# Summing 128 estimates on TensorE and turning a ternary weight once, from DRAM: a change to the last stages of a four-block transformer kernel

## The chip, the cores and the metric

The kernel runs on one core of one Trainium2 chip. The metric is the device time of the whole launch in microseconds; the median of 3 runs of the kernel before is 1473.65 us (1471.71 to 1474.03).

## The reference

Sixteen sequences of 256 tokens of width 512 pass four residual blocks: a strided cross attention, a sparse expert layer, a plain cross attention and a quantised feed-forward layer. Only the last block is touched by the change:

```python
def _quant_act_int8(x):
    amax = jnp.maximum(jnp.quantile(jnp.abs(x), 1.0 - 0.005), 1e-5)
    s = 127 / amax
    return jnp.clip(jnp.round(x * s), -128, 127) / s

def _quant_w_ternary(w):
    gamma = jnp.mean(jnp.abs(w)) + 1e-5
    return jnp.clip(jnp.round(w / gamma), -1.0, 1.0) * gamma

def _qlinear(x, w):
    return jnp.einsum('btd,hd->bth', _quant_act_int8(x), _quant_w_ternary(w))

h = _layernorm(x, ln_g, ln_b)          # 4096 tokens x 512
h = _qlinear(h, w1)                    # 4096 x 2048
h = jax.nn.gelu(h, approximate=False)
out = x + tanh(g_ffn[1]) * _qlinear(h, w2)   # 4096 x 512
```

The second product needs the 0.995 quantile of the magnitudes of all 8.4 million values of `h` before its input can be rounded. So the kernel first writes all of `h` to DRAM, finds the quantile, and reads `h` again.

## The kernel before

The program is a row of blocks. Each block gives every engine its own list of instructions, ordered among themselves by semaphores; between two blocks all engines meet, the semaphores are cleared, and all engines meet again (L111 to L113).

`product_tops` is the first product. 4096 tokens are 32 tiles of 128. PE (TensorE) works through 32 groups: 28 wide ones (two tiles by half of the 2048 columns, 32 matmuls of 256 columns) and 4 narrow ones (one tile by all columns). Group i writes bank i mod 2 of PSUM, and PE starts group i when ACT (ScalarE) has emptied group i-2 with its Gelu (L2025, L2027). The Gelu's output lands in one of three buffers of four tiles (`third` and two thirds of `hid`). From there SP's queue writes each tile to the DRAM tensor `activations` (1 MB, L1915), and DVE (VectorE) takes the largest 8 of every 1024 values of a partition into `cand` (16 MAX8 for each tile, L2067).

Three other things run inside this stage:

- SP first issues the transposing DMAs that give `qT`, the left operand (L1899).
- POOL (GpSimd) turns the second weight w2 (512 x 2048) into -1, 0, +1 in 8 half rows of 128 x 1024: two comparisons and a subtraction (L1957 to L1960), into `signs`, which is the space of `perm`. After each second half SP issues a transposing DMA of 128 x 2048 elements into `w2T` (`turn_w2`, L1906). It stands in SP's list behind the writing of tiles 13, 17, 21 and 25 (`W2_AFTER`) and waits there for POOL; POOL waits for the transfer to land before it fills `signs` again.
- ACT estimates the quantile while the product runs. After groups 9 to 19 (`EST_GROUPS`) it does one step of a binary search in each partition (L1977 to L1982). The 128 results, one for each partition in `minus_t`, are written by SP to the DRAM tensor `estimates` (L1920), and read back, all 128 into each partition, into `allest` (L1922). Both stand in SP's list behind the writing of tile 20. After group 23 (`MEAN_GROUP`) ACT waits for them, sums them (L1992) and works out a base point in six small instructions (`average`). DVE makes a grid of 256 thresholds out of it after tile 26 (`BASE_TILE`, L2072 to L2076), ACT takes their Gelu after group 28 (`GRID_GROUP`, L2004).

`quantile2` is the second search: eight rounds of counting `cand` against a threshold, by ACT (L2109) and DVE (L2122) at once; PE sums the counts. It uses no DMA. It gives `amax2` and a count that is checked later.

`ffn` with the prefix `p8_` is the second product: read a tile of `activations`, round it, multiply it by `w2T` (16 matmuls of 512 columns for each of 32 tiles, L2324), add the residual and write the output. It ends with a check of the quantile (L2329 to L2411) that leaves `flag`.

Behind it stand two blocks that do their work only if `flag` is set, which these inputs don't: `quantile2_of_all` (a search over all values) and `ffn` with the prefix `p9_`, unrolled in full. In each of them every engine loads the flag and branches over its list (`when`, L2227).

Of the kernel before, what the change touches and what calls it, by code (L numbers as in the profile page):

```python
# [1559 lines left out]
class Search:  # L1560
# [5 lines left out]
    def __init__(self, nc, es, name, K, integers=False, sems=None):  # L1566
# [8 lines left out]
        self.tot = es.enter_context(nc.psum_tensor(f"{name}_tot", [P, 512], F32))  # L1575
# [284 lines left out]
MEAN_GROUP = EST_GROUPS[-1] + 4  # L1860
# [3 lines left out]
W2_AFTER = (13, 17, 21, 25)  # L1864


def product_tops(nc, hid, qT, w1T, gam, amax, zs, Gs, g_d, cand, K, est_d, w2, th, nth, signs, room4, w2T, base, grid):
# [9 lines left out]
    with ExitStack() as es:  # L1877
# [4 lines left out]
        bits, steps, allest = sbt("bits", [P, IBITS]), sbt("steps", [P, IBITS]), sbt("allest", [P, P])  # L1882
# [6 lines left out]
                                        + "bits_in grid_in steps_done est_own est_done est_out est_in mean_done base_own base_done grid_done w_taken w_minus w_signed w_turned w_in0 w_in1".split()))  # L1889
# [5 lines left out]
        def _(sp):  # L1895
# [8 lines left out]
            def turn_w2(k):  # L1904
                sp.wait_ge(s["w_signed"], 2 * k + 2)
                sp.dma_start_transpose(w2T[:, :, k * P:(k + 1) * P], signs[:, :]).then_inc(s["w_turned"], 16)  # L1906

            turns = 0
            for n in range(NB * WB):
                while turns < min(NPAIR, 9 + 3 * (n // 2)):  # L1910
                    turn(turns)
                    turns += 1
                j, t = divmod(n, WB)
                sp.wait_ge(s["gelu_done"], ready[n])
                sp.dma_start(g_d[:, j, t], Gs[j % R][:, t]).then_inc(s[f"spilled{j % R}"], 16)  # L1915
                if n in W2_AFTER:
                    turn_w2(W2_AFTER.index(n))
                if n == EST_GROUPS[-1] + 1:
# [3 lines left out]
                    sp.dma_start(allest[:, :], est_d.rearrange("(a p) -> a p", a=1).broadcast_to([P, P])).then_inc(s["est_in"], 16)  # L1922
            sp.wait_ge(s["w_turned"], 16 * C)
# [4 lines left out]
        def _(pe):  # L1928
            for i, (n, tiles, f0, nf) in enumerate(groups):
# [5 lines left out]
                for f in range(nf):  # L1935
                    mm = z_product(pe, bank[:, f, :], w1T, qT, f0 + f, n, tiles)
# [3 lines left out]
        def _(pool):  # L1940
# [8 lines left out]
            for i in range(2 * C):  # L1949
# [3 lines left out]
                if k and h == 0:  # L1953
                    pool.wait_ge(s["w_turned"], 16 * k)
                if i:
                    pool.wait_ge(s["w_signed"], i)
# [3 lines left out]
                pool.tensor_tensor(half, half, below[:, :], ALU.subtract).then_inc(s["w_signed"], 1)  # L1960
                if i + 2 < 2 * C:
                    load(i + 2)

        @block.scalar
        def _(act):
# [49 lines left out]
            for i, (n, tiles, f0, nf) in enumerate(groups):  # L2015
# [17 lines left out]
                if i == MEAN_GROUP:  # L2033
                    average()
# [5 lines left out]
        def _(dve):  # L2040
# [9 lines left out]
            for k in range(NPAIR):  # L2050
# [3 lines left out]
                if k == 1:  # L2054
                    dve.tensor_scalar(zs[:, 0:1], amax[:, 0:1], 1.0 / QMAX, None, ALU.mult).then_inc(s["own"], 1)
                    own()
                    dve.tensor_tensor(zs[:, 0:1], zs[:, 0:1], gam[:, 0:1], ALU.mult).then_inc(s["scale_done"], 1)
            dve.memset(level[:, :], float(NT2 - 2 * int(rank_here) + 1))
# [20 lines left out]
def quantile2(nc, cand, K, zs, cut, small, amax, base, grid):  # L2079
# [5 lines left out]
    with ExitStack() as es:  # L2085
        sbt = lambda n, sh, d=F32: es.enter_context(nc.sbuf_tensor("q2_" + n, sh, d))
        s = es.enter_context(semaphores(nc, "qb_", "consts at_ready signed counted told own found gelu_done".split()))
# [6 lines left out]
        threshold = lambda i: grid[:, widths[i]:widths[i] + 1]  # L2094

# [46 lines left out]
def quantile2_of_all(nc, flag, rows, qT, w1T, K, zs, amax):  # L2142

    rank, _, low, high = quantile_ranks(N2)
    with ExitStack() as es:
        step_names = ("z_full", "gelu_done", "counted", "step_own")
        sems = es.enter_context(semaphores(nc, "qc_", [f"q2s_{n}" for n in Search.NAMES] + list(step_names)))
        slow = Search(nc, es, "q2s", K, sems=sems)
        junk = es.enter_context(nc.sbuf_tensor("q2s_junk", [P, TB], BF16))
        part = es.enter_context(nc.sbuf_tensor("q2s_part", [P, 1], F32))  # L2150
        bz = es.enter_context(nc.psum_tensor("q2s_z", [P, 512], F32))
        z_full, gelu_done, counted, step_own = [sems[n] for n in step_names]
        block = es.enter_context(nc.Block())
        g, mag = rows[:, 0, :], rows[:, 1, :]
        PER = NB * FC

        def chunks_of(eng, i, body):

            with eng.Fori(0, NB) as j:
                with eng.Fori(0, FC) as fc:  # L2160
                    body(j, fc, i * PER + j * FC + fc)

        @block.sync
        def _(sp):
            with when(sp, flag):
                slow.load(sp)

        @block.tensor
        def _(pe):
            with when(pe, flag):  # L2170
                pe.wait_ge(slow.s["const_in"], 32)
                m = Count(pe)

                def chunk(j, fc, before):

                    pe.wait_ge(counted, before + 1)
                    z_product(pe, bz[:, :], Sliced(w1T, fc), qT, 0, j * WB, WB).then_inc(z_full, 1)

                slow.answer(pe, m, lambda i: chunks_of(pe, i, chunk))

        @block.scalar
        def _(act):
            with when(act, flag):
                def chunk(j, fc, before):
                    act.wait_ge(z_full, before + 1)
                    act.activation(g, bz[:, :], ACT.Gelu, scale=zs[:, 0:1]).then_inc(gelu_done, 1)

                with act.Fori(0, BITS) as i:
                    chunks_of(act, i, chunk)

        @block.vector
        def _(dve):
            with when(dve, flag):
                dve.wait_ge(slow.s["const_in"], 32)
                m = Count(dve, slow.s["aside"])
                own = slow.s["own"]

                dve.sem_inc(counted, 1)
                dve.memset(slow.ones[:, :], 1.0).then_inc(own, 1)
                dve.wait_ge(own, m.next(own))  # L2200

                def count_all(i, trial, op):
                    dve.memset(slow.cnt[:, :], 0.0).then_inc(own, 1)
                    dve.wait_ge(own, m.next(own))
                    m.apart()

                    def chunk(j, fc, before):
                        dve.wait_ge(gelu_done, before + 1)
# [280 lines left out]
```

## Time and profile before

| | us |
|---|---|
| median of 3 runs | 1473.65 (1471.71 to 1474.03) |
| the profiled execution | 1465.63 |
| its span, first to last instruction | 1463.8 |

| engine | busy us | share of the span |
|---|---|---|
| PE | 1196.7 | 82% |
| PE weight loads | 887.8 | 61% |
| DVE | 952.1 | 65% |
| ACT | 702.7 | 48% |
| POOL | 454.7 | 31% |

One core is profiled by the hardware. A row of the timeline gives start, duration, engine, line, operation, output and input, a count where equal instructions are merged, and in brackets the idle time ahead of it with what ended it. "SPq" is SP's own queue of instructions, which issues DMAs; the duration of a DMA there is what the issue took, not the transfer. The granted clock of TensorE is given as a share of full speed: 1.00 is 2.4 GHz, 0.50 is 1.2 GHz. The DMA share is the mean busy share of the 16 DMA engines.

### The profile page before, as it was taken

How to read it: one execution, taken by the hardware profiler on the slowest of the kernel's cores; microseconds unless marked ns; L12 is line 12 of the kernel's file. 1: busy time of each engine (PE TensorE's matmuls, PEld its weight loads, DVE VectorE, ACT ScalarE, POOL GpSimd, SP SyncE). 2: the span in 40 equal slices, each digit the busy share in tenths (PEclk: the TensorE clock that was granted, in tenths of full speed). 3: DMA queues.
4: the chain of work that ended last, by engine and by line, in shares of the span. 5: the costliest groups of instructions: out<-in, count | busy, mean ns of one | idle time of the engine just before them, and what ended most of it. 6: DMA issues, size and time to landing. Idle time of an engine off the chain costs nothing. (4 is left out here: it accounts for less than half of the span.)

```text
span 1463.8 us, 25413 instructions
## 1 busy us (share of the span) xinstructions
PE 1196.7 (82%) x9166; PEld 887.8 (61%) x9166; DVE 952.1 (65%) x2244; ACT 702.7 (48%) x1139; POOL 454.7 (31%) x416
## 2 busy tenths in 40 slices
PE   6899999999999963899999399998141897425996
PEld 5788888888888852666664156555041686422443
DVE  5566777667677653344444279998486997366873
ACT  3233333434333321166444256766393784337991
POOL 1233333333333321011100136776200405702451
PEclk9999999999999986899999699999555899666998
DMA  5122222222222116869767899993300898744993
GB/s 207 44 87 103 74 73 73 79 94 89 98 72 73 52 58 215 312 224 323 276 232 288 322 376 317 335 331 115 135 1 1 187 367 262 211 187 154 418 356 108
DMA packets 117400, 268.17 MB, mean 183 GB/s; under 512 B 35729, under 2 KB 47153, under 8 KB 110641
## 3 DMA queue, kind: packets, MB, share of 16 engines
q1 hardware_dynamic: 103760, 228.98, 43.4%
q0 software_dynamic: 10560, 36.71, 8.0%
q10 hardware_dynamic: 2976, 1.14, 0.3%
q8 instruction: 60, 0.98, 0.3%
q14 instruction: 44, 0.35, 0.1%
HBM read 155.39 MB, written 105.12 MB: 178 GB/s over the span
## 5 line engine op out<-in xcount | busy, mean ns | idle before, releaser
L1847 PE MATMUL p_z<-qT,w1T 128*128 128x256 bf16 (+1 forms) x1152 | 116.2, 265 | 42.7 <-ACT third L2027 27.5
L1847 PEld LDWEIGHTS p_z<-qT,w1T 128*128 128x128 bf16 x1152 | 103.3, 99 | 55.5 <-issue 29.6
L923 PEld LDWEIGHTS p_sel<-p_pick,p_xp 128*128 128x128 bf16 x1536 | 89.3, 100 | 59.0 <-issue 34.2
L923 PE MATMUL p_sel<-p_pick,p_xp 128*128 128x128 bf16 x1536 | 100.6, 223 | 25.3 <-DVE p_pick L1045 12.5
L1061 DVE COPY p_selT<-p_sel 128x512 f32<-128x512 f32 x64 | 44.3, 692 | 104.2 <-PE p_sel L923 104.2
L2324 PE MATMUL p_o<-w2T,p_Gq 128*128 128x512 bf16 x384 | 85.7, 384 | 6.4 <-DVE p_Gq L2377 6.4
L1006 ACT ACTIVATE p_selT<-p_sel 128x512 f32<-128x512 f32 x64 | 38.2, 597 | 91.1 <-PE p_sel L923 91.1
L343 PE MATMUL p_M<-p_ctxTh,p_Wkh 128*128 128x256 f32 x256 | 75.8, 296 | 1.9 <-DVE p_Wkl L669 1.9
L343 PE MATMUL p_M<-p_xnTh,p_Wqh 128*128 128x256 f32 x256 | 75.0, 293 | 1.1 <-DVE p_V L742 1.1
L343 PE MATMUL p_M<-p_ctxTl,p_Wkh 128*128 128x256 f32 x256 | 72.9, 285 | 0.0
L343 PE MATMUL p_M<-p_ctxTh,p_Wkl 128*128 128x256 f32 x256 | 72.9, 285 | 0.0
L343 PE MATMUL p_M<-p_xnTh,p_Wql 128*128 128x256 f32 x256 | 72.0, 281 | 0.0
L343 PE MATMUL p_M<-p_xnTl,p_Wqh 128*128 128x256 f32 x256 | 71.9, 281 | 0.0
L2324 PEld LDWEIGHTS p_o<-w2T,p_Gq 128*128 128x128 bf16 x384 | 37.8, 99 | 52.6 <-DVE p_Gq L2377 6.4
L593 POOL TENSOR_TENSOR p_rs<-p_ve,p_mhalf 128x2 f32<-128x2 f32 x32 | 22.3, 697 | 150.8 <-DVE p_ve L659 150.7
L603 POOL TENSOR_TENSOR p_xb<-p_xin,p_tgbo 128x1024 f32<-128x1024 f32 x16 | 39.1, 2442 | 93.2 <-DVE p_sharedk L793 75.1
L513 ACT ACTIVATE p_qT<-p_M,p_bqT 128x256 f32<-128x256 f32 x64 | 26.9, 470 | 84.1 <-PE p_M L343 84.1
L2067 DVE MAX8 cand<-hid 128x8 f32<-128x128 f32 x320 | 62.6, 280 | 4.0 <-ACT hid L2027 4.0
L1255 PE MATMUL p_O<-p_cin,p_eT 128*128 128x512 f32 x128 | 62.6, 616 | 2.2 <-ACT p_eT L1323 2.2
L1730 PE MATMUL q_tot<-q_cnt,q_ones 128*128 128x4 f32 x32 | 9.3, 360 | 65.0 <-DVE q_junk L1780 32.9
L1237 PE MATMUL p_S<-p_ctxT,p_xnT 128*128 128x256 f32 x256 | 60.8, 380 | 0.2 <-ACT p_xnT L1309 0.2
L964 PE MATMUL p_lay<-p_f,p_inner 64*128 64x512 f32 x208 | 58.5, 638 | 2.8 <-DVE p_stage L1053 2.8
(335 smaller groups left out, 3450.7 us busy)
## 6 DMA issues: line engine op xcount, KB each, us to landing
inter_d<-p_stage SPq DMA_DIRECT2D x64, 512.0 KB, 4.3
p_rows<-inter_d SPq DMA_DIRECT2D x32, 1024.0 KB, 10.8
activations<-hid SPq DMA_DIRECT2D x20, 1024.0 KB, 10.0
p_cin<-in_ctx_dram SPq DMA_DIRECT2D x32, 512.0 KB, 5.4
xparts<-p_parts SPq DMA_DIRECT2D x16, 768.0 KB, 3.2
activations<-third SPq DMA_DIRECT2D x12, 1024.0 KB, 8.2
hid<-activations SPq DMA_DIRECT2D x12, 1024.0 KB, 14.9
p_xp<-xparts SPq DMA_DIRECT2D x3, 3072.0 KB, 25.2
```

Of the source, the lines that this page charges most:

```text
L343: mm = pe.matmul(out, left[a][:, c, lcols], right[e][:, c, rcols], start=(k == 0), stop=(k == len(terms) - 1))
L513: a = act.activation(dst[:, c, :], bM[k][:, (c % 2) * S:(c % 2 + 1) * S], ACT.Identity, bias=bias[:, c:c + 1])
L603: pool.tensor_tensor(xb[par][:, :, :], xin[par][:, :, :], tgbo[:, :].rearrange("p (a d) -> p a d", a=1).broadcast_to([P, NT, D]), ALU.add) ...
L923: mm = pe.matmul(bsel[u % 2][:, k * P:(k + 1) * P], xp[:, c, tile, r, :], pick[sb % 2][:, tile, :, :].rearrange("p s g -> p (s g)"), start ...
L964: mm = pe.matmul(bank(n, a)[:, :], inner[rows, j, h * P:(h + 1) * P], f2s[i // PAIRS][rows, j % (PAIRS // 2), :], start=True, stop=True)
L1006: act.activation(*picked(q, u), ACT.Copy).then_inc(s["sel_act"], 1)
L1061: dve.tensor_copy(*picked(q, u)).then_inc(s["sel_dve"], 1)
L1237: mm = pe.matmul(bS[:, t * S:(t + 1) * S], xnT[:, c, t * P:(t + 1) * P], ctxT[b % 2][:, c, :], start=(c == 0), stop=(c == C - 1))
L1255: mm = pe.matmul(bO[t][:, :], eT[:, k, t, :], cin[b % CD][:, k, :], start=(k == 0), stop=(k == NT - 1))
L1847: mm = pe.matmul(bank, w1T[:, c, fc * P:(fc + 1) * P], qT[:, bass.ds(first, tiles), c, :], start=(c == 0), stop=(c == C - 1))
L2067: a = dve.max(cand[:, c:c + 8], Gs[j % R][:, t, :, k * OCT:(k + 1) * OCT])
L2324: mm = pe.matmul(bo[n % len(bo)][:, :], Gq[n % QR][:, k, :], w2T[:, k, :], start=(k == 0), stop=(k == FC - 1))
```

## The change

1. The estimates are summed by PE. PE waits ahead of group 21 for the last estimate, multiplies a matrix of ones by `minus_t` into one column of the bank of group 21, and does the group's column blocks in the order 2, 3, ..., 0, 1, so that the blocks that share the bank's first part with the sum come last; ahead of block 0 it waits until ACT has read the sum. `MEAN_GROUP` becomes 21, `average` runs after group 20, `BASE_TILE` becomes 24 and `GRID_GROUP` 26. The tensor `estimates` and SP's two DMAs of it go.
2. `turn_w2` leaves SP's list. POOL writes each ternary half row (128 x 1024 bf16, 256 KB) with a DMA of its own queue to the DRAM tensor `ternary2` and waits, before it uses a half of `signs` again, for its write only. In `quantile2` SP issues one transposing DMA of all 512 x 2048 elements from DRAM into `w2T`, and waits for it inside that block.
3. The general part moves into the block of the second product: every engine waits for the flag at the end of its list there, loads it once and branches over one body (`Redo`), in which the second product is a loop over tiles. The blocks `quantile2_of_all` and `p9_` are gone. SP waits for all stores of the output at its end.

The diff, cut to its core:

```diff
-MEAN_GROUP = EST_GROUPS[-1] + 4
+MEAN_GROUP = EST_GROUPS[-1] + 2
 BASE_TILE = MEAN_GROUP + 3
 GRID_GROUP = BASE_TILE + 2
-W2_AFTER = (13, 17, 21, 25)
 ...
                 sp.dma_start(g_d[:, j, t], Gs[j % R][:, t]).then_inc(s[f"spilled{j % R}"], 16)
-                if n in W2_AFTER:
-                    turn_w2(W2_AFTER.index(n))
-                if n == EST_GROUPS[-1] + 1:
-                    sp.wait_ge(s["est_done"], 1)
-                    sp.dma_start(est_d.rearrange("(p a) -> p a", a=1), minus_t[:, :]).then_inc(s["est_out"], 16)
-                    sp.wait_ge(s["est_out"], 16)
-                    sp.dma_start(allest[:, :], est_d...broadcast_to([P, P])).then_inc(s["est_in"], 16)
-            sp.wait_ge(s["w_turned"], 16 * C)
 ...
-                for f in range(nf):
+                if i == MEAN_GROUP:
+                    pe.wait_ge(s["est_done"], 1)
+                    pe.matmul(bz[i % 2][:, 0:1], ones[:, :], minus_t[:, :], start=True, stop=True).then_inc(s["est_summed"], 1)
+                for f in list(range(2, nf)) + [0, 1]:
+                    if i == MEAN_GROUP and f == 0:
+                        pe.wait_ge(s["est_read"], 1)
                     mm = z_product(pe, bank[:, f, :], w1T, qT, f0 + f, n, tiles)
 ...
-                if k and h == 0:
-                    pool.wait_ge(s["w_turned"], 16 * k)
+                if i >= 2:
+                    pool.wait_ge(s[f"w_out{i % 2}"], 16 * (i // 2))
 ...
                 pool.tensor_tensor(half, half, below[:, :], ALU.subtract).then_inc(s["w_signed"], 1)
+                pool.wait_ge(s["w_signed"], i + 1)
+                pool.dma_start(w2t_d[k * P:(k + 1) * P, h * HW:(h + 1) * HW], half).then_inc(s[f"w_out{i % 2}"], 16)
 ...
-                act.wait_ge(s["est_in"], 16)
-                act.activation(compared[:, 0:P], allest[:, :], ACT.Copy, scale=-1.0 / P, accum_out=mean[:, :]).then_inc(s["est_own"], 1)
-                own()
+                act.wait_ge(s["est_summed"], 1)
+                act.activation(mean[:, :], bz[MEAN_GROUP % 2][:, 0:1], ACT.Copy, scale=-1.0 / P).then_inc(s["est_read"], 1)
+                act.wait_ge(s["est_read"], 1)
 ...
-                if i == MEAN_GROUP:
+                if i == MEAN_GROUP - 1:
                     average()
 ...
+        @block.sync      # in quantile2
+        def _(sp):
+            sp.dma_start_transpose(w2T[:, :, :], w2t_d).then_inc(s["w_turned"], 16)
+            sp.wait_ge(s["w_turned"], 16)
 ...
+        def again(eng, body):      # in ffn, last in the list of PE, ACT, DVE and SP
+            eng.wait_ge(s["flag_done"], 1)
+            with eng.If(eng.value_load(flag[0:1, 0:1], min_val=0, max_val=1) > 0):
+                body(eng)
 ...
+        def product(n):            # TensorE's part of Redo, run in m.loop(0, NB * WB, product)
+            pe.wait_ge(s["r_q"], m.next(s["r_q"]))
+            for k in range(FC):
+                mm = pe.matmul(self.bo[:, :], self.Gq[:, k, :], self.w2T[:, k, :], start=(k == 0), stop=(k == FC - 1))
+            mm.then_inc(s["r_o"], 1)
 ...
-    quantile2_of_all(nc, flag, room, qT, w1T, K, zs, amax2)
-    ffn(nc, "p9_", Gs, spare, perm, g_d, w2T, gam, amax2, gf, x3_d, out_d, flag=flag)
```

## Rows read from the trace of the kernel before

**Rows 1.** The chain that ended last: start us, us, what.
```profile
1339.10 112.17 PE p_o L2324 x512
...
1452.19 0.40 PE p_o L2329 x2
...
1452.80 0.16 DVE flag L2411
```

**Rows 2.** Waits, 1000 to 1465 us: total us, times, longest us.
```profile
POOL perm L1957 <- DMA w2T<-perm: 57.8, 3, 43.1
ACT p_compared L1992 <- DMA p_allest<-estimates: 28.4, 1, 28.4
```

**Rows 3.** Windows: length; PE, PEld, DVE, ACT, POOL busy; clock, DMA share, GB/s.
```profile
1200.00:1210.00 10.00, 10.00 (x94) 8.97 (x92) 8.58 (x45) 9.60 (x14) 0.00 (x0) 1.00 1.00 410
1240.00:1250.00 10.00, 0.00 (x0) 0.00 (x0) 0.00 (x0) 0.00 (x0) 9.49 (x5) 0.50 0.74 256
1260.00:1270.00 10.00, 7.13 (x47) 5.58 (x48) 5.39 (x28) 5.88 (x6) 5.10 (x2) 0.65 1.07 370
1290.00:1300.00 10.00, 0.00 (x0) 0.00 (x0) 4.21 (x22) 0.00 (x0) 0.00 (x0) 0.55 0.89 371
```

**Rows 4.** Timeline of SP's queue, 1140 to 1465 us.
```profile
1232.78 4.58 SPq L1906 DMA_TRANSPOSE w2T<-perm  x1
...
1239.59 1.22 SPq L1920 DMA_DIRECT2D estimates<-p_minus_t  x1
...
1280.86 1.33 SPq L1906 DMA_TRANSPOSE w2T<-perm  x1
...
1283.43 5.30 SPq L1915 DMA_DIRECT2D activations<-hid  x4
```

**Rows 5.** Timeline of ACT, 1150 to 1345 us.
```profile
1217.58 0.39 ACT L1982 ACTIVATE p_minus_t<-p_higher,p_minus_t,p_steps 128x1 f32<-128x1 f32 x1
1218.32 1.97 ACT L2027 ACTIVATE hid<-p_z,zs 128x2048 f32<-128x2048 f32 x1 [0.36 <-PE p_z L1847]
1221.51 1.97 ACT L2027 ACTIVATE hid<-p_z,zs 128x2048 f32<-128x2048 f32 x1 [1.22 <-PE p_z L1847]
...
1228.50 1.97 ACT L2027 ACTIVATE hid<-p_z,zs 128x2048 f32<-128x2048 f32 x1 [1.53 <-PE p_z L1847]
1258.83 0.31 ACT L1992 ACTIVATE p_compared<-p_allest 128x128 bf16<-128x128 f32 x1 [28.36 <-DMA p_allest<-estimates]
...
1286.42 1.97 ACT L2025 ACTIVATE hid<-p_z,zs 128x2048 f32<-128x2048 f32 x1 [1.60 <-PE p_z L1847]
```

**Rows 6.** Timeline of DVE, 1150 to 1345 us.
```profile
1281.78 12.43 DVE L2067 MAX8 cand<-hid 128x8 f32<-128x128 f32 x64
1302.48 0.17 DVE L2116 MEMSET q_half<- 128x128 f32 x1 [8.27 <-PEq L113]
...
1334.12 0.16 DVE L2138 TENSOR_TENSOR small<-small,q_lowest 128x1 f32<-128x1 f32 x1
```

**Rows 7.** Waits of SP's queue, 1130 to 1305 us.
```profile
SPq L1925 <- DMA activations<-hid: 12.2, 1, 12.2
```

**Rows 8.** DMA issues, 1280.5 to 1285 us, median us to landing; then all writes (L1915).
```profile
w2T<-perm SPq DMA_TRANSPOSE x1, 3.7
```
```profile
DMA to landing us min/median/max: 4.3/8.9/16.1
```

**Rows 9.** Timeline of POOL, 1130 to 1345 us.
```profile
1156.32 2.86 POOL L1957 TENSOR_SCALAR perm<-cand,th 128x1024 bf16<-128x1024 f32 x1 [21.11 <-DVE hid L2053]
...
1222.15 2.12 POOL L1960 TENSOR_TENSOR perm<-perm,p_below 128x1024 bf16<-128x1024 bf16 x1
```

**Rows 10.** Queue instructions of L2249, L2227 and L113: ns min/median/max, first and last start.
```profile
L2249 SPq EVENT_SEMAPHORE  x2: 17/17/17, 1454.4 to 1462.7; - x2
```
```profile
L2227 PEldq COMPARE_BRANCH  x2: 213/2026/3839, 1456.3 to 1458.6; - x2
```
```profile
L113 PEldq EVENT_SEMAPHORE  x9: 51/51/51, 566.2 to 1463.7; - x9
```

More of the change, by code:

```diff
@@ L2139, in _ @@
             dve.wait_ge(s["found"], 4)
[L2142 to L2208, printed above, removed]
-                        dve.scalar_tensor_tensor(mag, g, -1.0, g, ALU.mult, ALU.max).then_inc(step_own, 1)
-                        dve.wait_ge(step_own, before * 2 + 1)
-                        dve.tensor_scalar(junk[:, :], mag, trial, 0.0, op, ALU.add, accum_out=part[:, :]).then_inc(step_own, 1)
-                        dve.wait_ge(step_own, before * 2 + 2)
-                        dve.tensor_tensor(slow.cnt[:, :], slow.cnt[:, :], part[:, :], ALU.add).then_inc(counted, 1)
-                        dve.wait_ge(counted, before + 2)
-                    chunks_of(dve, i, chunk)
-                    dve.tensor_copy(slow.cnt[:, :], slow.cnt[:, :]).then_inc(slow.s["asked"], 1)
-                slow.find(dve, m, count_all, rank)
-                slow.finish(dve, m, amax, (low, high))
@@ L2238, in __getitem__, with ffn @@
         return self.w[p, c, bass.ds(self.first, P)]
-def ffn(nc, prefix, Gs, spare, perm, g_d, w2T, gam, amax, gf, x3_d, out_d, flag=None, check=None):
-    cut, small, rank, flag_out = check or (None,) * 4
+def ffn(nc, Gs, spare, perm, g_d, w2T, gam, amax, gf, x3_d, out_d, cut, small, flag, rows, qT, w1T, zs, K):
+    rank, prefix = quantile_ranks(N2)[0], "p8_"
     R, QR, LAG, YR, BEHIND = len(Gs), 4, 4, 8, 2
@@ L2267, in ffn @@
         token_tile = lambda n: order[n // WB] * WB + n % WB
-        first = RES if check else 0
         def arrived(eng, n):
             k = n % SLOTS
-            if n >= first:
-                eng.wait_ge(s[f"g_in{k}"], 16 * (n // SLOTS + (0 if check and k < RES else 1)))
-        by_act = lambda n: n % 2 == 0 and not (check and n == 0)
+            if n >= RES:
+                eng.wait_ge(s[f"g_in{k}"], 16 * (n // SLOTS + (0 if k < RES else 1)))
+        by_act = lambda n: n % 2 == 0 and n > 0
@@ L2331, in _ @@
+            pe.wait_ge(s["asked"], 1)
+            pe.wait_ge(s["y_done"], WB * NB)
+            pe.matmul(bo[0][:, 0:1], ones[:, :], total[:, :], start=True, stop=True).then_inc(s["told"], 1)
+            again(pe, redo.on_tensor)
         @block.scalar
         def _(act):
[L2333 to L2345 removed]
+            act.wait_ge(s["scales"], 1)
@@ new lines, in _ @@
+            for n in range(NB * WB):
+                integers(n)
+                if n == LAG - 1:
+                    combined()
+                if n >= LAG:
+                    output(n - LAG)
+            for n in range(NB * WB - LAG, NB * WB):
+                output(n)
+            dve.tensor_reduce(total[:, :], cnt[:, :], AX.X, ALU.add).then_inc(s["asked"], 1)
+            dve.wait_ge(s["told"], 1)
+            dve.tensor_scalar(worse[:, :], bo[0][:, 0:1], float(2 * rank - N2), None, ALU.is_ge).then_inc(own, 1)
@@ L2417, in feed_forward @@
+            dve.wait_ge(own, n_.next(own))
+            dve.tensor_tensor(flag[:, :], worse[:, :], small[:, :], ALU.max).then_inc(s["flag_done"], 1)
+            again(dve, redo.on_vector)
+def feed_forward(nc, es, room, spare, qT, w1T, w2T, gam, amax1, gf, K, x3_d, g_d, w2t_d, out_d, w2, th, nth, perm):
     sbt = lambda n, s, d=F32: es.enter_context(nc.sbuf_tensor(n, s, d))
```

317 lines of the change are left out of this document (183 added, 134 removed).

## The prediction, written before the changed kernel was run

> **What bounds the kernel now.** I read the page's table of engines first: PE is busy for 82% of the span, so a place where PE stands still is where time can be won. Then the chain of waits that ended last: it reaches back only through the second product (112.17 us of PE) and ends with the flag at 1452.96 us [rows 1]. The span is 1463.8 us, so 10.8 us follow in which nothing is computed. The list of waits over the last stages names the largest stall of an engine that matters: ACT waits 28.4 us, once, for `allest` [rows 2]. The windows show what hangs on it: from 1240 to 1250 us neither PE, DVE nor ACT does anything, and the granted clock is 0.50; from 1260 to 1270 us PE is back, at a mean clock of 0.65 [rows 3].
>
> SP's timeline tells why ACT waits. The last estimate is ready at 1217.97 us [rows 5], but SP stands at the second `turn_w2`, which waits for POOL, and issues it at 1232.78 us and the estimates at 1239.59 us [rows 4]. The write and the reading back, queued behind 1 MB tiles, come in at 1258.83 us [rows 5]. POOL was late because it waited itself for transposing DMAs, 43.1 us the first time [rows 2]. So the two things that the change takes from SP's list form one knot.
>
> The end of the stage is bound by something else. The last Gelu starts at 1286.42 us and ends at 1288.4 [rows 5], DVE's last MAX8 ends at 1294.2 us [rows 6], and SP waits 12.2 us for the last writes [rows 7], until 1300.9 us: seen in the DMA share of 0.89 from 1290 to 1300 us [rows 3]. Those writes are late because the fourth `turn_w2` held SP until 1280.86 us; the last four tiles then left within 5.3 us [rows 4]. The second search starts at 1302.5 us.
>
> **Part 1, the sum on PE.** Removed: the stall. From the Gelu of group 23 (1228.50) to that of group 31 (1286.42) it is 57.92 us for eight groups [rows 5]. Undisturbed, a wide group takes 3.49 us (1221.51 to 1228.50 are two groups [rows 5]); a narrow one has twice the matmuls of half the width, and I give it 3.6. Four of each make 28.3 us. So 29.6 us go, a little more than the wait, since the slow clock behind it goes too.
>
> Added on PE: one product of 128 x 128 by one column in f32. The nearest instruction is the check's sum at the end, of the same shape: 0.40 us [rows 1]. I take 0.5. The wait for the estimate costs nothing: ACT has it at 1217.97 us, and PE ends group 20 only at 1218.3, which is when its Gelu starts [rows 5]. The wait ahead of block 0 is for ACT: Gelu of group 20 until 1220.3, then one small copy, so about 1220.6. PE reaches block 0 after the sum and six of eight blocks, 1218.8 + 2.6 = 1221.4: hidden by 0.8 us. If that cover is gone, PE loses the difference once, a microsecond. `average` costs ACT some 1.8 us once where it has 1.5 us to spare in a group (3.49 - 1.97): 0.1 us at most, which I put into rounding. The grid moves two groups forward and keeps its distances. DVE takes 12.43 us for four tiles [rows 6], 3.1 for one against PE's 3.49, keeps up, and pays 1.5 us for the base as before. Net: 29.0 us. The last Gelu ends at 1259.4.
>
> **Part 2, w2.** SP's list has only writes left once `qT` is done. The last tile is issued when its Gelu ends, 1259.4. Its landing lies between 4.3 us (the fastest of 32) and 16.1 (the slowest), median 8.9 [rows 8]. The slow ones came in bunches behind a held SP. A tile each 3.5 us is 300 GB/s where 410 GB/s were moved at a share of 1.00 [rows 3], so a backlog melts; POOL's own traffic (2 MB of writes more, its loads as before) comes on top, but POOL is soon through: a half row is two comparisons of 2.86 and a subtraction of 2.12 us [rows 9], with two issues some 9.5 us, and eight of them from 1156.3 on end at about 1232. After that the queue has 27 us to drain. I take 7 us, so the writes end at 1266.5. DVE ends at about 1264.5: from its last tile's Gelu 1259.4 plus 3.1 us, and 2 us of lag behind the base. The stage ends at 1266.5 against 1300.9: **34.4 us**. Bounds: 36.4 us with DVE last, 25.4 us with a landing of 16.1 us.
>
> The transposing DMA moves beside the second search, 1302.5 to 1334.3 us, 31.8 us in which no other DMA runs [rows 6]. The row that prices it: one of 128 x 2048 from SBUF, on a queue that was empty, landed in 3.7 us [rows 8]; four of them in sequence are 14.8 us, and as one stream less. From DRAM no row shows one. Below: not less than zero on the path, since the block must be passed anyway. Above: 31.8 us are free, which is twice the 14.8. I cost it at nothing. What it costs if this cover is gone is the excess over 31.8 us, in full, because SP waits for it inside the block and all engines meet there.
>
> The Trainium skill speaks against it, in "DMA: Bandwidth & Descriptors", "Why small descriptors are slow (HBM only)": small descriptors pay a penalty at HBM that SBUF-to-SBUF traffic is spared, and its "Specifications" ask for 512 B or more. No row here shows a transposing DMA from DRAM. If the rule made it twice as slow, 14.8 us would be 29.6 as an estimate, and the sum would stay, by 2 us.
>
> **Part 3, the end.** Before, the second product's block closes at 1454.4 us. The last block closes at 1462.7 and its barriers and clearing end at 1463.7 [rows 10], so I give the first 1.0 us too: 1455.4. The two blocks behind it cost 8.3 us; of these 3.84 us are one branch of PE, over the unrolled 512 matmuls, while the same branch over the short body of the search took 0.21 us [rows 10]. After, the flag's load and test (0.7 us) start at 1452.96 and end beside the last output's landing (1454.4). PE's new body holds the search and 32 matmuls (16 peeled, 16 in the loop). It is nearer to the short one, so I take 0.3 us net: **8.0 us**. If it took 3.84 us, the branch would end at 1457.5, 3.0 us too late: 5.3 us.
>
> The Trainium skill, "Runtime: NRT & Kernel Launch", "Instruction fetch mechanics", says that a taken branch whose target is outside the pages at hand stalls for a fetch; the two branches of this trace (0.21 and 3.84 us) agree. By that rule PE's branch here could still be a slow one, and the sum would be 3 us less.
>
> **The sum.** 34.4 + 8.0 = 42.4 us. The profiled execution took 1465.63 us, 8.0 less than the median of the runs; nothing in the trace tells why, and I carry the gain over as it is: 1423.2 for a profiled one, **1431.3 us** for the median.
>
> **Rivals.**
> (a) The writes bind the end of the stage. For: the share was 1.00 between 1200 and 1210 us [rows 3], and POOL's writes add to it. Against: 300 GB/s needed, 410 seen. Landing 10 to 16 us after the last Gelu, gain 25 to 31 us there and 5.3 to 8 at the end: 1435 to 1443 us.
> (b) The transposing DMA outlasts the search. For: DRAM as a source is not in the trace, and it is one instruction over 512 rows. Against: a factor of 2.1 over the SBUF row is needed before it is seen. At 50 us it costs 18 us: 1449 us.
> (c) Slower than before: the same mechanism, further. It decides from 31.8 + 42.4 = 74 us on, five times the SBUF rows' 14.8; at 100 us the excess is 68.2 us and the time 1431.3 + 68.2 = 1499.5 us.
> (d) The change doesn't do what it says: ACT stalls at the sum all the same, because the estimate or PE is later than I read. Only the drained queue and the end would be won, 8 to 13 us: about 1463 us.
>
> **How the numbers follow.** Forecast as summed 0.62, (a) 0.20, (b) 0.08, (c) 0.05, (d) 0.03, a remainder of 0.02 no change. The forecast's own range is 1426 to 1437: 36.4 + 8.3 at best, 5.3 at the end at worst, and 2 us of scatter of a median. For 8 in 10 it must take in (a): 1424 to 1446. A measurement of this kernel can tell about 0.2% (3 us) from no change. Faster by more: 0.62 + 0.20 + 0.08 + 0.03 = 0.93; within: 0.02; slower: 0.05.
>
> **What would show it.** In the profile after: no wait for `allest` and none of over 2 us on ACT between groups 19 and 24; PE's product as one piece at clock 1.00; ACT's last Gelu near 1257 us; SP's wait behind the product under 8 us; the second search starting near 1268 us; one transposing DMA landing before its end and no wait for it; the last barrier 2.6 to 3 us behind the flag. The forecast is wrong if SP's wait in the second search ends the block, if SP's wait for the writes is over 12 us again, or if PE's branch is the last thing before the final barrier.

## The result, and the profile after

| | before | after |
|---|---|---|
| median of the runs beside each other | 1473.4 us (1471.7 to 1474.0) | 1432.8 us (1430.6 to 1434.4) |
| ratio of the medians | | 0.9725, 95% interval 0.9708 to 0.9743 |
| profiled execution, time / span | 1465.63 / 1463.8 us | 1434.06 / 1432.3 us |
| PE busy | 82% of the span | 84% |

The kernel is 2.7% faster. The forecast was 1431.3 us, in a range of 1424 to 1446. The total came out; one term of its sum, the landing of the last writes, did not, and the profile taken with the result hides that, as the experiments show.

The list of ACT's waits of after, from 1130 to 1280 us (us in total, times, longest us), has no `allest` any more. The line that answers to the 28.4 us of [rows 2] is gone, and a smaller stall has come up, for `qT`:

```profile
ACT p_q L2004 <- DVE hid L2047: 18.8, 4, 17.6
ACT q_junk_a L2109 <- DVEq L2120: 9.2, 1, 9.2
ACT p_q L2004 <- DMA qT<-p_q: 8.6, 2, 7.6
```

ACT's timeline of after (start us, us, instruction, in brackets the idle time before it and what ended it) shows that stall at 1180.94 us, the sum at its place behind the Gelu of group 20, and the last Gelu; it answers to [rows 5]:

```profile
1180.94 1.06 ACT L2004 ACTIVATE p_q<-hid 128x1024 bf16<-128x1024 f32 x1 [7.65 <-DMA qT<-p_q]
...
1190.02 1.97 ACT L2021 ACTIVATE hid<-p_z,zs 128x2048 f32<-128x2048 f32 x1 [3.22 <-PE p_z L1847]
...
1228.81 1.97 ACT L2021 ACTIVATE hid<-p_z,zs 128x2048 f32<-128x2048 f32 x1 [0.36 <-PE p_z L1847]
1230.67 0.16 ACT L1986 ACTIVATE p_mean<-p_z 128x1 f32<-128x1 f32 x1
...
1232.58 1.97 ACT L2021 ACTIVATE hid<-p_z,zs 128x2048 f32<-128x2048 f32 x1 [0.25 <-PE p_z L1847]
...
1267.81 1.97 ACT L2019 ACTIVATE hid<-p_z,zs 128x2048 f32<-128x2048 f32 x1 [1.61 <-PE p_z L1847]
```

Between the Gelus of groups 20 and 21 lie 3.77 us where [rows 5] has 3.19 (1218.32 to 1221.51): the sum costs 0.6 us, once. PE's timeline shows the product, and ahead of it a short wait for the last estimate:

```profile
1228.59 0.35 PE L1924 MATMUL p_z<-p_minus_t,p_ones 128*128 128x1 f32 x2 [0.19 <-ACT p_minus_t L1976]
```

The windows of after (length; PE, PEld, DVE, ACT, POOL busy; clock, DMA share, GB/s) answer to [rows 3]. Where PE stood at a clock of 0.50 it is now busy throughout at 1.00. The DMA share, though, is still 1.01 between 1250 and 1260 us:

```profile
1240.00:1250.00 10.00, 10.00 (x94) 8.96 (x93) 8.61 (x45) 5.45 (x3) 0.00 (x0) 1.00 1.02 424
1250.00:1260.00 10.00, 10.00 (x153) 9.66 (x151) 9.92 (x52) 6.41 (x4) 0.00 (x0) 1.00 1.01 421
1260.00:1270.00 10.00, 7.71 (x139) 7.54 (x136) 10.00 (x54) 5.90 (x3) 0.00 (x0) 1.00 0.98 404
```

SP's queue has only writes left before the end of the stage, and then the one transposing DMA (timeline of SP, answering to [rows 4]); below it, from the list of SP's waits, the writes behind the product (12.2 us in [rows 7]) and the transposing DMA:

```profile
1259.11 11.02 SPq L1910 DMA_DIRECT2D activations<-hid  x4
1278.21 7.76 SPq L2093 DMA_TRANSPOSE w2T<-ternary  x1
```
```profile
SPq L1912 <- DMA activations<-hid: 6.4, 1, 6.4
SPq L2080 <- DMA w2T<-ternary: 2.1, 1, 2.1
SPq L2080 <- PEq L2080: 22.4, 1, 22.4
```

The transposing DMA is issued at 1278.2 us, landed 9.8 us later, and SP then has nothing to do for 22.4 us until the block ends. At the end of the program the flag, last in the chain that ended last (it answers to [rows 1]), is 3.5 us ahead of the end of the span where it was 11.0. The queue's instructions (ns min/median/max, first and last start; answering to [rows 10]) name PE's branch, now 0.33 us, and the last barrier at 1432.2 us:

```profile
1428.78 0.16 DVE flag L2443
```
```profile
L2311 PEldq COMPARE_BRANCH  x1: 329/329/329, 1430.0 to 1430.0; - x1
```
```profile
L113 PEldq EVENT_SEMAPHORE  x7: 51/51/51, 566.3 to 1432.2; - x7
```

### The profile page after: what moved, and what is told of

Its sections match the earlier page's. It is cut to its first block and busy times, and to the rows that moved or that the text cites. A ratio compares the mean times of both kernels' runs of the same rounds, so it can differ in the third digit from the quotient of the medians.

```text
span 1432.3 us, 25333 instructions
## 1 busy us (share of the span) xinstructions
PE 1199.1 (84%) x9168; PEld 889.7 (62%) x9168; DVE 953.7 (67%) x2245; ACT 702.5 (49%) x1138; POOL 460.7 (32%) x424
## 5 line engine op out<-in xcount | busy, mean ns | idle before, releaser
L2062 DVE MAX8 cand<-hid 128x8 f32<-128x128 f32 x320 | 62.7, 280 | 13.4 <-ACT hid L2021 13.4
L603 POOL TENSOR_TENSOR p_xb<-p_xin,p_tgbo 128x1024 f32<-128x1024 f32 x16 | 39.1, 2444 | 92.1 <-DVE p_sharedk L793 75.1
L2346 POOL DMA_DIRECT2D p_y<-residual x32 | 29.8, 935 | 98.5 <-POOLq L113 72.4
## 6 DMA issues: line engine op xcount, KB each, us to landing
activations<-third SPq DMA_DIRECT2D x12, 1024.0 KB, 12.2
```

Of the source, the lines that this page charges most:

```text
L603: pool.tensor_tensor(xb[par][:, :, :], xin[par][:, :, :], tgbo[:, :].rearrange("p (a d) -> p a d", a=1).broadcast_to([P, NT, D]), ALU.add) ...
L2062: a = dve.max(cand[:, c:c + 8], Gs[j % R][:, t, :, k * OCT:(k + 1) * OCT])
L2346: pool.dma_start(y[n % YR][:, :], x3_d[:, token_tile(n), :]).then_inc(s[f"x_in{n % YR}"], 16)
```

## The experiments

Two questions were open. First, does each part do what the sum says, and why did the profiled execution gain only 31.6 us where the sum said 42.4? Second, what ends the first product's stage now?

**The kernel before again, and each part alone.**

> The kernel before, unchanged, profiled once more. Its profiled execution took 1465.6 us and the median of its runs 1473.4, 7.8 us more; the kernel after shows no such gap (1434.1 profiled, 1432.8 median). Theory A: an execution of either kernel can have or lack a stall of 7 to 9 us in which a transposing DMA of qT is late (the kernel after has it in its profile, ACT waits 7.65 us for qT; the first profile of before has 2.0 us there). Then this profile shows either about 1465 without it or about 1473 with such a wait. Theory B: the gap comes from elsewhere (start, end or clock): the wait for qT stays at 2 us whatever the time.

Measured: 1468.3 us in the profiled execution, and 1465.6 to 1474.7 us in 13 runs of the same kernel beside it. The stall was there again (`ACT p_compared L1992 <- DMA p_allest<-estimates`, 30.3 us), and no long one for `qT` (1.5 us at most). 1468.3 us lies between the two times that theory A allows, so this profile leaves A and B undecided. The kernel before scatters over 9 us, and the profile on which the prediction rests, 1465.63 us, lay at the lower end.

The sum alone: `SP` no longer writes and reads the estimates, all of `turn_w2` stays.

```
-                if n == EST_GROUPS[-1] + 1:
-                    ...
-                    sp.dma_start(allest[:, :], est_d...broadcast_to([P, P]))
+                if i == MEAN_GROUP:
+                    pe.wait_ge(s["est_done"], 1)
+                    pe.matmul(bz[i % 2][:, 0:1], ones[:, :], minus_t[:, :], ...)
```

> Part 1 alone: the sum by TensorE, group numbers as after; the turning of w2 stays in SP's list. Theory A (one knot): the stall of ACT (28.4 us) is gone, but SP still stands at the fourth turning of w2 until about 1281 us, because POOL and SP wait for each other; six tiles are written behind it and the stage ends at about 1297 to 1300 us as before. Time 1468 to 1473 us. Theory B (the parts add): the stall is worth its 28 us by itself: about 1445 us.

Measured: 1468.6 us, ratio 0.9984 [0.9968, 1.0]. The whole stall of 28 us is gone, and 2 us are won, 5 at most by the interval. ACT's and SP's timelines, and two of the waits, show why:

```profile
1258.02 1.97 ACT L2026 ACTIVATE hid<-p_z,zs 128x2048 f32<-128x2048 f32 x1 [1.60 <-PE p_z L1847]
1300.72 2.21 ACT L2111 ACTIVATE q_junk_a<-cand,grid 128x2304 bf16<-128x2304 f32 x1 [40.74 <-DVEq L2122]
```
```profile
1279.82 1.60 SPq L1907 DMA_TRANSPOSE w2T<-perm  x1
1281.46 1.06 SPq L1916 DMA_DIRECT2D activations<-third  x2
1282.57 5.14 SPq L1916 DMA_DIRECT2D activations<-hid  x4
```
```profile
SPq L1907 <- POOL perm L1961: 47.7, 3, 16.7
SPq L1921 <- DMA activations<-hid: 10.8, 1, 10.8
```

The last Gelu starts at 1258.0, as in the forecast for the whole change, and then ACT waits 40.7 us for the second search. SP stands at the fourth `turn_w2` until 1279.8 us, in front of the last six writes, and this comes out as theory A has it. The stall of ACT had run beside this one.

The second weight alone: no `turn_w2`, `ternary2` through DRAM, one transposing DMA in `quantile2`; the estimates still go through DRAM.

```
-                if n in W2_AFTER:
-                    turn_w2(W2_AFTER.index(n))
+                pool.dma_start(w2t_d[k * P:(k + 1) * P, h * HW:(h + 1) * HW], half)...
+            sp.dma_start_transpose(w2T[:, :, :], w2t_d).then_inc(s["w_turned"], 16)
```

> Part 2 alone: the ternary weight through DRAM, turned in the second search; the estimates still pass through DRAM behind tile 20. Theory A: SP is free when the estimate is there; what is left of the 28.4 us is writing and reading back behind 1 MB tiles (14.5 + 4.7 us at worst) less the 10 us until group 23 needs it: a wait of 5 to 12 us. Time 1450 to 1458 us. Theory B (the round trip through DRAM was the stall, not SP's place in the queue): the wait stays over 20 us, time over 1462 us.

Measured: 1451.1 us, ratio 0.9865 [0.9843, 0.9887]. From SP's timeline and the waits:

```profile
1224.91 1.05 SPq L1913 DMA_DIRECT2D estimates<-p_minus_t  x1
1245.24 0.32 SPq L1915 DMA_DIRECT2D p_allest<-estimates  x1
```
```profile
ACT p_compared L1986 <- DMA p_allest<-estimates: 16.6, 1, 16.6
```

Without POOL's knot the estimates leave at 1224.9 us, but a write of 0.5 KB takes 20 us behind the tiles of 1 MB in the same queue, and ACT still waits 16.6 us. The time fell in the expected range; the wait was larger than expected, so the queue behind 1 MB writes is by itself an important part of what the sum on PE removes. Theory A holds in the time and not in its 5 to 12 us of waiting.

The end alone: `Redo` inside the second product's block, from the change.

```
-    quantile2_of_all(nc, flag, room, qT, w1T, K, zs, amax2)
-    ffn(nc, "p9_", Gs, spare, perm, g_d, w2T, gam, amax2, gf, x3_d, out_d, flag=flag)
```

> Part 3 alone: one body for the general part inside the second product's block. The two blocks behind the flag go: 7.5 us (the profile after has 3.4 us from flag to end, before 10.9). Time 1465 to 1467 us by either theory; if it is 1473 the end's gain is hidden in the launch.

Measured: 1460.9 us, ratio 0.9932 [0.9909, 0.9956], 9.7 us less; the flag at 1452.4 us stands 3.5 us ahead of the end of the span. By the profile the end gives 7.5 us; the medians say 2 us more, which is within the interval (6.5 to 13.4 us).

Singly the parts give 2.0, 19.6 and 9.7 us, 31 in all; together they give 41. The last of this set asks where the other 10 are.

```
     (the change, with the end of the program as before)
+    quantile2_of_all(nc, flag, room, qT, w1T, K, zs, amax2)
+    ffn(nc, "p9_", ..., flag=flag)
```

> The estimates' sum by TensorE and the second weight through DRAM together, with the end of the program as it was (the general part in blocks of its own). One by one the three edits gave 2.0, 19.6 and 9.7 us, 31 in all, and together 41. Theory K (the missing 9 us are one knot: each of the first two leaves the other's stall in place, the end has nothing to do with it): 7.5 to 10 us slower than the change, 1438 to 1442 us, so that the two give about 31 us together where they gave 22 singly. Rival E (the end gains more in company, because the blocks behind a slower product cost more): the two give about 22 us, 1448 to 1451 us.

Measured: 1439.6 us (1435.2 to 1441.9), ratio 0.9807 [0.9777, 0.9836]: 29 us for the two, where singly they gave 22. So a surplus lies between the sum and the second weight, as theory K says: each leaves the other's stall in place, and only both undo the knot. Its size is loosely known: from the three intervals I estimate 7 us, give or take 6. The mechanism rests on the traces, the 47.7 us that SP still waits for POOL with the sum alone, and the 16.6 us that ACT still waits with the weight alone.

**The change again.**

> The kernel after, unchanged, as the partner of the other three in this call. In its first profile ACT waited 7.65 us for a late transposing DMA of qT at 1173 us, and everything behind stood 9 us later than forecast; with part 2 alone, which has the same DMAs on POOL's queue, the profile showed no such wait. Theory S (systematic): POOL's writes and loads of w2, mixed with the 256-byte packets of SP's transposing DMAs, cause it; it is here again. Theory R (chance of an execution): it may be absent, and the time is then about 1425 us. Forecast by S: 1430 to 1434 us.

Measured: 1429.8 us (1427.8 to 1434.3), ratio 0.973 [0.9709, 0.9751]. The profiled execution took 1428.8 us, and the stall for `qT` was not there; from its timelines of ACT and DVE, and SP's waits:

```profile
1257.43 1.97 ACT L2019 ACTIVATE hid<-p_z,zs 128x2048 f32<-128x2048 f32 x1 [1.61 <-PE p_z L1847]
1273.91 2.21 ACT L2109 ACTIVATE q_junk_a<-cand,grid 128x2304 bf16<-128x2304 f32 x1 [14.52 <-DVEq L2120]
```
```profile
1273.26 0.17 DVE L2116 MEMSET q_half<- 128x128 f32 x1 [9.49 <-PEq L113]
```
```profile
SPq L1912 <- DMA activations<-hid: 11.7, 1, 11.7
```

The last Gelu starts 10.4 us earlier than in the first profile, at 1257.4 as forecast. The search starts only 5 us earlier: SP waits 11.7 us for the writes, and DVE stands for 9.5 us. The windows of this profile show the queue full until the last Gelu:

```profile
1240.00:1250.00 10.00, 10.00 (x156) 9.70 (x155) 9.92 (x52) 6.05 (x4) 0.00 (x0) 1.00 1.02 425
1250.00:1260.00 10.00, 7.33 (x132) 7.16 (x129) 10.00 (x53) 5.90 (x3) 0.00 (x0) 1.00 1.01 423
```

**Do POOL's DMAs make the turns of `qT` late?** In the first profile the issues of three turns stretch over 15.9 us, from 1173.7 to 1189.5 us, with a DMA share of 1.37 for only 78 GB/s:

```profile
1173.65 15.86 SPq L1898 DMA_TRANSPOSE qT<-p_q  x3
```
```profile
1175.00:1180.00 5.00, 2.33 (x22) 1.84 (x19) 1.45 (x8) 0.00 (x0) 1.17 (x3) 1.00 1.37 78
```

Three kernels keep POOL's traffic away from them. In the first, POOL begins only when all of `qT` is turned (`pool.wait_ge(s[f"turned{i}"], ...)` ahead of its loop):

> After, with POOL's whole work on w2 held until the last transposing DMA of qT has landed (about 1190 us); only the first two loads of w2, issued 20 us before, overlap with the turns, as before. Theory S: the wait for qT falls to 2 us or less and the Gelu of group 9 starts at about 1180 instead of 1190; but POOL then needs 76 us from 1190 on, to 1266, and its last write lands at about 1272, behind the last tile's write (1267 to 1270): net gain 3 to 6 us against the kernel after. Theory R: no gain, 0 to 5 us slower, as POOL ends late.

Measured: 1433.1 us (1426.1 to 1436.8), ratio 0.9745 [0.9719, 0.977].

In the second, POOL's first four writes are left out, and two writes of the last rows, of the same bytes together, stand at the end in their place. This kernel so leaves out rows 0 to 255 of the ternary weight, half of the second product's right operand; its time is used here, its output is not that of the reference:

```
-                pool.dma_start(w2t_d[k * P...
+                if i >= LEFT:
+                    pool.dma_start(w2t_d[k * P...
```

> After, with the first four of POOL's eight writes to DRAM taken away from the time of the turns of qT: two writes of the whole of signs (the last rows) at POOL's end stand in their place, so the ternary weight has wrong rows 0 to 255; bytes are the same, the loads of w2 stay where they are. Theory S1 (the writes slow the turns): wait for qT at 2 us, 7 to 9 us faster than the kernel after. Theory S2 (the loads do): like the kernel after within 2 us. Theory R: like the kernel after on the average of the runs, with or without the wait in the profile.

Measured: 1428.4 us (1423.0 to 1430.3), ratio 0.9711 [0.9685, 0.9737].

In the third, POOL computes two half rows at once, but holds its DMAs until the turns are over:

> After, with only POOL's DMAs held: it works out the first two half rows as before (1157 to 1173 us), then waits for the last turn of qT (about 1190), issues the two writes and two loads, and goes on; POOL's arithmetic stays 17 us ahead of b1 and should end at about 1250, well before the product. Theory S: the wait for qT falls to 2 us or less, 7 to 9 us faster than the kernel after, about 1424 us. Theory R: within 2 us of it.

Measured: 1432.0 us (1427.8 to 1433.2), ratio 0.9735 [0.9716, 0.9755]. None differs from the change by more than the intervals. The longest wait of ACT for `qT` was 0.8, 2.1 and 1.3 us in the three, but in the change's own second profile there was none of 0.5 us or more. Five further profiles of kernels in this document have POOL's DMAs beside the turns as in the change, and none has the long wait (3.4 us in all at most). Theory S, that POOL's DMAs cost the turns 9 us each time, falls: the long stall is a chance of single executions. What makes it is not known; the first profile shows only that turns and DRAM traffic were in flight together. The unusual item is one single issue: SP stood 11.0 us at the first of the three turns, where the longest issue of a turn took 4.5 us in the second profile and 3.9 to 6.3 us in those of all other kernels here.

The three show something else. In each the last Gelu is long over when the stage ends. The time from the end of the last Gelu to the end of the stage (the search's first DVE instruction, less the 1.62 us that it starts behind the end of DVE's work where nothing else is waited for, as in the kernel below, less the Gelu's end) is:

| kernel | last Gelu ends | stage ends | between |
|---|---|---|---|
| the change, first profile | 1269.8 | 1276.7 | 6.9 us |
| the change, second profile | 1259.4 | 1271.6 | 12.2 us |
| POOL behind the turns | 1262.0 | 1274.7 | 12.7 us (POOL last) |
| first writes last | 1259.6 | 1269.1 | 9.5 us |
| DMAs held | 1259.1 | 1270.8 | 11.7 us (POOL last) |

In both profiles of the change and with the first writes last, SP's wait for its writes is the last thing (0.2 us more until the others are there). In the other two POOL, which the edit makes late, comes 2.5 and 0.7 us behind SP; for the first of them SP's list of waits has

```profile
SPq L1876 <- PEq L1876: 2.5, 1, 2.5
```

Without POOL the writes of SP would have ended these stages too, 10.2 and 11.0 us behind the last Gelu. Between the two profiles of the change the last Gelu moved by 10.4 us and the end of the stage by 5.1: half of what the product lost was absorbed, because the queue had its own work to finish.

**Does the backlog of writes end the stage?** The last four tiles' writes move into the second search's block, behind the transposing DMA, where SP has 22 us left over.

```
-            for n in range(NB * WB):          # product_tops, SP
+            for n in range(NB * WB - 4):
 ...
             sp.dma_start_transpose(w2T[:, :, :], w2t_d)...   # quantile2, SP
+            for n in range(NB * WB - 4, NB * WB):
+                sp.dma_start(g_d[:, j, t], Gs[j % len(Gs)][:, t]).then_inc(s["last_out"], 16)
```

> The changed kernel, with the DMAs that write its last four tiles of activations (1 MB each) moved from the first product's block into the second search's: SP issues them behind the transposing DMA and waits for them there, where it had 22 us left over; every byte is still written. Theory W (in undisturbed executions the first product's block ends with the landing of its writes, which took about 13 us behind the last Gelu instruction where the forecast took 7): SP's wait behind the product falls from 7.8 to 11.7 us to under 3 us, the block ends about 6 us behind the start of the last Gelu instruction, by the last MAX8, and the second search starts about 8 us behind that start instead of 11 to 16 us; the time falls by 3 to 8 us to 1422 to 1428 us. Rival T (the transposing DMA of 2 MB and four writes of 1 MB don't fit beside the search): the search starts early as in W, but SP's waits end its block, and the time stays at 1430 us or rises. Rival X (the wait of SP only runs beside the real end, that of ACT and DVE): the search doesn't start earlier against the last Gelu instruction, and the time is 1429 to 1434 us.

Measured: 1423.6 us (1419.9 to 1427.0), ratio 0.9696 [0.9671, 0.9721]. ACT's and DVE's timelines, SP's timeline and its waits:

```profile
1256.21 1.97 ACT L2020 ACTIVATE hid<-p_z,zs 128x2048 f32<-128x2048 f32 x1 [1.61 <-PE p_z L1847]
1264.82 2.21 ACT L2114 ACTIVATE q_junk_a<-cand,grid 128x2304 bf16<-128x2304 f32 x1 [6.64 <-DVEq L2125]
```
```profile
1250.12 12.44 DVE L2063 MAX8 cand<-hid 128x8 f32<-128x128 f32 x64
1264.17 0.17 DVE L2121 MEMSET q_half<- 128x128 f32 x1 [1.62 <-PEq L113]
```
```profile
1264.06 7.70 SPq L2094 DMA_TRANSPOSE w2T<-ternary  x1
1271.81 3.41 SPq L2097 DMA_DIRECT2D activations<-hid  x4
```
```profile
SPq L2081 <- PEq L2081: 12.8, 1, 12.8
SPq L1877 <- DMA activations<-third: 10.8, 1, 10.8
SPq L2081 <- DMA activations<-hid: 8.2, 1, 8.2
SPq L1877 <- PEq L1877: 5.5, 1, 5.5
```

DVE's last MAX8 ends at 1262.56 us and the search starts 1.6 us behind it: now DVE ends the stage, 4.4 us behind the last Gelu. SP still waits 10.8 us for the writes that are left in the stage, and not under 3 us as theory W had it; but it is through 5.5 us ahead of the others. The last four writes land inside the search, and SP has 12.8 us left even so. Theory W holds in what ends the stage and in the time. Once more, for the size:

> The kernel with the last four writes behind the transposing DMA once more, for the size of what it gains over the change: its ratio to the kernel before was 0.9696 [0.9671, 0.9721], that of the change 0.9725 and 0.973 [0.9709, 0.9751], and the two intervals just touch. Theory W (the landing of the writes bound the block's end): 0.967 to 0.971 again, SP's wait behind the product under 3 us, and the second search starting 8 us behind the start of the last Gelu instruction, whatever the execution lost before it. If the gain was a chance of its call: 0.972 to 0.974, 1430 us or more.

Measured: 1423.4 us (1417.9 to 1427.4), ratio 0.9684 [0.9658, 0.9711]. In its profile the last Gelu started 4 us later, at 1260.27 us, and ACT's gap to the search was 6.64 us again. The eleven runs of this kernel have a median of 1423.4 us (1417.9 to 1427.4), the nine of the change 1430.6 (1427.8 to 1434.4): no run of one lies among those of the other. The two were not run beside each other, though, and the kernel before was 2 to 5 us faster beside this kernel (medians 1468.5 and 1469.8 us) than beside the change (1473.4 and 1471.4). By the ratios (0.9696 and 0.9684 against 0.9725 and 0.973) the late writes gain some 5 to 6 us over the change, and not the whole 7 us between the medians.

**How much room the transposing DMA has.**

```
-            sp.dma_start_transpose(w2T[:, :, :], w2t_d).then_inc(s["w_turned"], 16)
-            sp.wait_ge(s["w_turned"], 16)
+            for k in range(4):
+                sp.dma_start_transpose(w2T[:, :, :], w2t_d).then_inc(s["w_turned"], 16)
+                sp.wait_ge(s["w_turned"], 16 * (k + 1))
```

> The changed kernel, with its transposing DMA of the second weight issued four times, one behind the other. One landed 9.9 us after its issue, so four take about 40 us where SP's wait leaves 32 us free: by the reading that this DMA is hidden and has 22 us to spare, SP's wait, not the search, ends the block, 7 to 9 us later than before, and the time is 1437 to 1442 us. If instead the later ones run faster than the first, whose start is shared with the writes of the product, 1430 to 1436 us. If the reading that it is hidden is wrong and each DMA is paid for in full, 30 us more: 1462 us.

Measured: 1437.3 us (1435.9 to 1438.0), ratio 0.9783 [0.9753, 0.9812]. SP's timeline, and where DVE stands at the end of the search:

```profile
1275.07 37.12 SPq L2094 DMA_TRANSPOSE w2T<-ternary  x4
```
```profile
1306.88 0.16 DVE L2139 TENSOR_TENSOR small<-small,q_lowest 128x1 f32<-128x1 f32 x1
1315.47 0.06 DVE L2394 MEMSET p_magic<- 128x1 f32 x1 [8.44 <-PEq L113]
```

With the last one's 2.0 us until landing, the four take 39.1 us, 9.8 each, and DVE waits 8.44 us where it waits 1.36 in the change: 7.1 us are paid, of 29 us added. So the DMA is hidden, costs the path only what goes over the search's length, and all of that.

## Why the prediction was right, and where it was not

**The stall of ACT goes, and with it 29 us.** Right. The last Gelu was forecast to start at 1257.4 us and started at 1257.43 in the second profile, at 1258.0 with the sum alone. The pieces hold as well. From the Gelu of group 23 to that of group 31 it took 28.3 us in both profiles of the change, as forecast. The sum on PE cost 0.6 us, which is what was taken (0.5 for the product and 0.1 in rounding); the wait for the estimate, which had been put at nothing, was 0.2 us, and 0.5 in the second profile. That the last Gelu's start agrees to some hundredths is luck: ACT began the stage 1.4 us later than in the profile of before (1136.57 against 1135.13 us), and then did not wait for `qT`, where before it waited 2.9 us in all. In the first profile the last Gelu came at 1267.8: it was 1.5 us behind the second profile ahead of the chance stall for `qT` and 10.7 behind it, so the stall cost 9.2. The forecast had no place for that.

**The writes' landing, taken as 7 us.** This is the term that was mis-sized. It measured 6.9 us only where the Gelus themselves were 10 us late; where they were on time it was 9.5 to 12.2 us (12.2 in the change). The failed step is "the queue has 27 us to drain": POOL was to be through at 1232, and its last write left at 1235.04 us in the second profile, 1238.88 in the first; and the share of 1.02 and 1.01 at 425 and 423 GB/s from 1240 to 1260 us in the second profile shows that the backlog had not melted by then. The arithmetic of 300 GB/s needed against 410 moved left out what was in the queue already. It also took POOL's own traffic for done once POOL was: in a queue that never runs empty, 2 MB more are 4.9 us more at 424 GB/s, by my estimate nearly the whole miss of 5.2; no run leaves these writes out. So the landing of rival (a), 10 to 16 us, is what happens, at its low end; it had been given 0.20, and its time of 1435 us and more did not come. Two of the signs named beforehand say the same in the second profile: SP's wait behind the product was to be under 8 us and was 11.7, just short of the 12 that were to refute the forecast, and the search was to start near 1268 us and started at 1273.3. Only the kernel with the late writes reaches the bound with DVE last, 4.4 us behind the last Gelu.

**The transposing DMA costs nothing.** Right, with 22.4 us of room. It landed in 9.8 us, against 14.8 estimated as four times the 3.7 of the SBUF source, and 31.8 free. Windows in which a transposing DMA moved alone, from SBUF in the kernel before and from DRAM in the change, show one rate for both, 285 and 290 GB/s:

```profile
1282.10:1283.40 1.30, 1.30 (x27) 1.30 (x25) 1.30 (x8) 0.56 (x1) 0.00 (x0) 1.00 1.25 285
```
```profile
1281.00:1287.00 6.00, 2.00 (x8) 1.85 (x8) 3.54 (x11) 2.89 (x5) 0.00 (x0) 0.50 1.27 290
```

At that rate the 0.5 MB of the row are 1.8 us (an estimate), so about 2 us of its 3.7 are not spent moving, against 2.6 of the 9.8 for four times the bytes; the forecast counted them four times. The Trainium skill's objection, "DMA: Bandwidth & Descriptors", "Why small descriptors are slow (HBM only)", weighed as an estimate of 29.6 us, does not show: the DMA from DRAM, in pieces of 256 B, moved as fast as the one from SBUF. Rivals (b) and (c) asked for 32 and 74 us; four in a row took 39.1 and cost 7.1, so their mechanism is real, and far away.

**The end, 8.0 us.** 7.5 by the profile (11.0 to 3.5 us behind the flag). PE's branch took 0.33 us, not 3.84. The Trainium skill, "Runtime: NRT & Kernel Launch", "Instruction fetch mechanics", would have allowed a slow branch here too; none was seen.

**The sum.** For the second profile it closes: 1423.2 forecast, plus 5.2 for the landing (12.2 less 7) and 0.5 for the end is 1428.9, and it took 1428.8. Against the profile on which the forecast rests, the gain is 36.9 us, not 42.4. That the median still came out, at 40.6 and 41.5 us of gain, is in part luck: the profile of before lay 8 us below its median, and the forecast carried its gain over unchanged. The change's profiles lie around its median (1434.1 and 1428.8 against 1432.8 and 1429.8). The 4 to 5 us by which the medians differ more than these profiles cancelled most of the 5.2 us of the landing, and why they differ stays open. The long runs of before are those with the lower mean clock (1474.65 us at 0.896, 1465.58 us at 0.905, with the others between them nearly in order); whether the clock is the cause or goes down with PE's waiting is not shown.

**The pieces against each other.** Not forecast as such, but read rightly as "one knot": the sum alone gives 2 us for a stall of 28, since the stalls ran side by side. Rival (d) and no change did not occur.

## What to carry to other kernels

Before a stall is counted as a gain, look for what else stands still during it: here removing 28 us of waiting alone gave 2 us, because SP was held for another reason over the same time, and both had to go.

Here the DMA share stood at 1.0 for the last 60 us of the product, and the writes landed 12 us behind the last Gelu. Where a trace shows such a stretch, look for a backlog: count the bytes still to be moved over the whole stretch at the rate of the saturated windows, rather than take the landing time of one DMA. Price what a change adds to that traffic by the same count. Work whose end nobody needs yet, as the last writes here, belongs behind the next barrier, beside a stage in which the queue is idle.

One profile is one execution: when it stands at the edge of the runs, say by how much, and look at a second one before a difference of that size is explained.

## What the runs showed of the hardware

- A transposing DMA of the 2 MB ternary matrix out of DRAM landed in 9.8 us, four in a row in 39.1 us. One of 128 x 2048 from SBUF, a quarter of it, took 3.7 us [rows 8]. Moving alone both ran at 285 to 290 GB/s.
- A write of 512 bytes took 13.3 us (before) and 19.3 us (with the second weight alone) of SP's waiting behind writes of 1 MB on the same queue.
- While turns of `qT` and DRAM traffic were in flight together the DMA share read 1.37 at 78 GB/s: the engines were taken up and moved a fifth of what they move otherwise (421 GB/s at 1.01). The stall that went with this stretch cost 9 us in one execution of the change; the next had no such stall.
- PE's branch over the loops of the general part took 0.33 us, against 3.84 us over 512 unrolled matmuls [rows 10].
